# Exponentials per head straight from PSUM, and transpositions that alternate with first-layer products, in a gated cross-attention and feed-forward kernel

## The reference

```python
x = x + tanh(g_xattn[0]) * attention(layernorm(x), ctx)     # 8 heads of 64, 77 keys
x = x + tanh(g_ffn[0]) * ffn(layernorm(x))                  # 256 -> 1024 -> 256, fixed point

attn = softmax(einsum('bhnd,bhmd->bhnm', q, k) * scale)     # over the 77 keys
def quantized_linear(x, w, b):   # x rounded to 1/16, w and b to 1/64, clipped to 8 bits
    return einsum('bsi,oi->bso', xq, wq) + bq
h = relu(fixed_quant(quantized_linear(x, w1, b1)))
out = quantized_linear(h, w2, b2)
```

## Time and profile before

| | us |
|---|---|
| median of 3 runs (lowest, highest) | 119.74 (119.52, 121.28) |
| the profiled execution's own time | 120.01 |
| its span | 118.2 |
| TensorE busy | 111.8 |
| VectorE busy | 97.7 |
| GpSimd busy | 89.1 |
| ScalarE busy | 76.4 |

### The profile page before, as it was taken

How to read it: one execution, slowest core, us unless ns; L and a number is a source line. 1 busy time by engine, 2 the same in 40 slices (tenths; PEclk the granted TensorE clock), 3 DMA queues, 4 the chain that set the end, 5 groups by cost and what they waited for, 6 DMA issues and landing times.

```text
span 118.2 us, 2898 instructions
## 1 busy us (share of the span) xinstructions
PE 111.8 (95%) x1012; PEld 102.1 (86%) x1012; DVE 97.7 (83%) x223; ACT 76.4 (65%) x169; POOL 89.1 (75%) x161
## 2 busy tenths in 40 slices
PE   7979997899999999999999999999999999999990
PEld 2659976899798999988999999999999999897870
DVE  3029798999999999989999999999797979648981
ACT  4137766869688894998667575748483819448420
POOL 4003587698796989898989978996899999988720
PEclk9999999999999999999999999999999999999999
DMA  4989799300000000000010002000200020020204
GB/s 80 315 247 386 280 375 399 152 0 8 0 3 0 6 3 0 0 6 0 0 74 15 6 0 89 0 3 6 89 0 0 3 89 6 0 89 8 88 13 165
DMA packets 5328, 8.87 MB, mean 75 GB/s; under 512 B 1191, under 2 KB 2242, under 8 KB 5186
## 3 DMA queue, kind: packets, MB, share of 16 engines
q1 hardware_dynamic: 5082, 8.34, 20.1%
q10 hardware_dynamic: 232, 0.34, 0.9%
HBM read 6.59 MB, written 2.10 MB: 73 GB/s over the span
## 4 chain that ended last, share of the span: by engine, by line
PE 52%; POOL 21%; DVE 14%; DMA 5%; issue 3%; ACT 1%; SPq 1%; POOLq 0%; DVEq 0%; ACTq 0%
PE sc_ps L841 15%; PE of_ps L878 12%; PE h_ps L910 7%; DMA wq_sb<-in_L_xattn_Wq_dram 5%; POOL hid L362 5%; POOL x_sb L383 4%; PE of_ps L925 4%; POOL probs L300 4%; POOL rstd L310 3%; POOL yq L316 3%; DVE probs L614 3%; PE tr_ps L853 3%; DVE mx L609 3%; DVE den L621 2%; DVE pT L650 1%
## 5 line engine op out<-in xcount | busy, mean ns | idle before, releaser
L841 PE MATMUL sc_ps<-a_sb,xT 128*128 128x308 f32 x192 | 31.1, 311 | 0.7 <-DVE probs L614 0.7
L878 PE MATMUL of_ps<-u_sb,pT 128*128 128x256 f32 x240 | 30.9, 281 | 0.1
L878 PEld LDWEIGHTS of_ps<-u_sb,pT 128*128 128x128 f32 x240 | 29.5, 188 | 0.3 <-issue 0.3
L841 PEld LDWEIGHTS sc_ps<-a_sb,xT 128*128 128x128 f32 x192 | 27.4, 188 | 1.4 <-issue 1.2
L438 ACT ACTIVATE probs<-probs,rstd 128x616 f32<-128x616 f32 x16 | 13.1, 818 | 23.0 <-DVE probs L614 23.0
L481 ACT ACTIVATE hid_q<-h_ps,b1z 128x256 int8<-128x256 f32 x58 | 24.5, 494 | 3.6 <-PE h_ps L910 3.6
L300 POOL TENSOR_TENSOR probs<-probs,rden 128x616 f32<-128x616 f32 x16 | 19.5, 1221 | 1.9 <-DVE rden L624 1.9
L362 POOL CAST hid<-hid_q 128x512 bf16<-128x512 int8 x27 | 15.8, 611 | 2.0 <-ACT hid_q L481 2.0
L910 PE MATMUL h_ps<-x2T,w1T 128*128 128x256 bf16 x128 | 16.7, 274 | 0.0
L609 DVE TENSOR_REDUCE mx<-sc_ps 128x8 f32<-128x616 f32 x16 | 12.6, 787 | 2.8 <-PE sc_ps L841 2.7
L614 DVE TENSOR_TENSOR probs<-sc_ps,mx 128x616 f32<-128x616 f32 x16 | 12.8, 800 | 0.5
(11 more groups left out here) (124 smaller groups left out, 175.8 us busy)
## 6 DMA issues: line engine op xcount, KB each, us to landing
w_sb<-in_L_ffn_w_dram SPq DMA_DIRECT2D x2, 1024.0 KB, 10.9
out_dram<-x_sb SPq DMA_DIRECT2D x7, 256.0 KB, 2.5
x_sb<-in_x_dram SPq DMA_DIRECT2D x4, 256.0 KB, 8.0
x_sb<-in_x_dram SPq DMA_DIRECT2D x1, 1024.0 KB, 9.8
wq_sb<-in_L_xattn_Wq_dram SPq DMA_DIRECT2D x1, 512.0 KB, 5.8
wv_sb<-in_L_xattn_Wv_dram SPq DMA_DIRECT2D x1, 512.0 KB, 7.8
wo_sb<-in_L_xattn_Wo_dram SPq DMA_DIRECT2D x1, 512.0 KB, 8.6
wk_sb<-in_L_xattn_Wk_dram SPq DMA_DIRECT2D x1, 256.0 KB, 3.4
```

What stands on the lines that cost most here:

```text
L841: ins = nc.tensor.matmul(sc_ps[:, a, 0:HALF], xT[:, T % 2, p, c, :], a_sb[:, q, T // TB, c, HALF * a:HALF * a + HALF], start=first, stop=last)
L878: ins = nc.tensor.matmul(attn_ps, pT[:, T % 2, p, P * c:P * c + P], u_sb[:, q, MC * (T // TB) + c, :], start=first, stop=last)
```

## The change

Two things are changed.

First, from slot 4 on, the five transpositions of `probsT(s)` no longer stand ahead of the eight products of `hidden(s-4)`: a transposition and a product take turns, and the last three products follow together.

Second, for tiles 2 to 15 without 5 (`HEAD_EXP`), VectorE no longer subtracts the maximum. It writes minus maximum times `rstd1` (8 columns), and ScalarE takes the exponential of each head's 77 scores from PSUM with this as bias and `rstd1` as scale, eight activations for a tile. `sc_ps` is then free when the exponentials are done, so `scores` of the next tile waits for `exp_done`. In these tiles `center(s+2)` stands ahead of `stats_first(s+5)` on VectorE, no longer behind it.

```diff
+HEAD_EXP = tuple(T for T in range(2, TILES) if T != 5)
...
             def exponentials(T):
                 act.wait_ge(rstd1_ready, T + 1)
-                act.wait_ge(centered, T + 1)
-                nc.scalar.activation(probs_v(T), probs_v(T), ACT.Exp, scale=rstd1[:, T:T + 1]).then_inc(exp_done, 1)
+                if T in HEAD_EXP:
+                    act.wait_ge(minus_max_ready, T + 1 - centered_by(T))
+                    act.wait_ge(pT_psum, T - 1)
+                    for h in range(H):
+                        ins = nc.scalar.activation(probs_v(T)[:, h, :], sc_v[:, h // 4, h % 4, :], ACT.Exp,
+                                                   bias=minus_max[:, T % 2, h:h + 1], scale=rstd1[:, T:T + 1])
+                    ins.then_inc(exp_done, 1)
+                else:
+                    act.wait_ge(centered, centered_by(T))
+                    nc.scalar.activation(probs_v(T), probs_v(T), ACT.Exp, scale=rstd1[:, T:T + 1]).then_inc(exp_done, 1)
...
+                if T in HEAD_EXP:
+                    dve.wait_ge(rstd1_ready, T + 1)
+                    nc.vector.tensor_scalar(minus_max[:, i, :], mx[:, i, :], rstd1[:, T:T + 1], -1.0, ALU.mult,
+                                            ALU.mult).then_inc(minus_max_ready, 1)
+                    return
...
+                if s + 2 in HEAD_EXP:
+                    center(s + 2)
                 if 1 <= s and live(s + 5):
                     stats_first(s + 5, s + 6)
-                if live(s + 2):
+                if live(s + 2) and s + 2 not in HEAD_EXP:
                     center(s + 2)
...
             def scores(T):
                 pe.wait_ge(xT_high, T + 1)
-                if T >= 1:
-                    pe.wait_ge(centered, T)
+                if T - 1 in HEAD_EXP:
+                    pe.wait_ge(exp_done, T)
+                elif T >= 1:
+                    pe.wait_ge(centered, centered_by(T - 1))
...
-            def hidden(k):
+            def hidden(k, probs_of=None):
                 p, half = k // 2, k % 2
+                if probs_of is not None:
+                    probsT_waits(probs_of)
+                    transposed_chunk(probs_of, 0)
...
-                    ins.then_inc(hid_psum, 1)
+                            if (c, d) == (1, DK - 1):
+                                ins.then_inc(hid_psum, 1)
+                            done = 4 * n + 2 * c + d + 1
+                            if probs_of is not None and done < MC:
+                                transposed_chunk(probs_of, done)
...
-                probsT(s)
+                if s >= 4:
+                    hidden(s - 4, probs_of=s)
+                else:
+                    probsT(s)
```

More of the change, by code:

```diff
@@ L123, in flamingo_kernel @@
         mx = sb("mx", [P, 2, H])
+        minus_max = sb("minus_max", [P, 2, H])
         probs_words, probs = words_of("probs", [P, 2, HMP])
@@ L225, in flamingo_kernel @@
         scores_ready, max_ready, centered, exp_done = sem("scores_ready"), sem("max_ready"), sem("centered"), sem("exp_done")
+        minus_max_ready = sem("minus_max_ready")
         den_ready, rden_ready, probs_ready = sem("den_ready"), sem("rden_ready"), sem("probs_ready")
@@ L238, in flamingo_kernel, with centered_by @@
         block = stack.enter_context(nc.Block())
+        def centered_by(T):
+            return len([t for t in range(T + 1) if t not in HEAD_EXP])
         def live(T):
@@ L845, in probsT, with probsT_waits @@
             def probsT(T):
+                probsT_waits(T)
+                for c in range(MC):
+                    transposed_chunk(T, c)
+            def probsT_waits(T):
                 pe.wait_ge(probs_ready, T + 1)
@@ L851, in probsT, with transposed_chunk @@
                 pe.wait_ge(xT_ready, min(T + 3, TILES))
[L852 to L855, removed]
+            def transposed_chunk(T, c):
+                ins = nc.tensor.transpose(pT_ps[:, P * c:P * c + P].bitcast(F32R), probs_words[:, T % 2, P * c:P * c + P],
+                                          ident_r[:, :])
+                if c == MC - 1:
+                    ins.then_inc(pT_psum, 1)
             def attend(T):
@@ L887, in quantisedT @@
                 else:
-                    pe.wait_ge(centered, TILES)
+                    pe.wait_ge(exp_done, TILES)
                     if T - 2 in yT_last:
@@ L1022, in _ @@
                     output_weights(1)
-                if s >= 4:
-                    hidden(s - 4)
                 if s == 5:
```

## The result

The changed kernel takes 131.64 us (median of 4 runs, 130.87 to 134.52) against 119.63 before: 1.099 times the time, 95% interval 1.094 to 1.104. The forecast was slower, 126.3 us, range 122.0 to 129.5. The direction was right, and so was the circle that the prediction describes (maximum, exponentials, denominators, next maximum); the size was not: the loss is 12.0 us, forecast 6.7.

The account below looks back on a forecast made before the run. TensorE bounds the kernel from 36.45 to near 80 us, VectorE before, GpSimd after to 109.0; the change closes a circle. 120.01 + 6.5 (13 steps 6.1, tail 0.4) = 126.5, median 126.3 us, range 122.0 to 129.5.

Parts of the forecast that it names:

- the circle: VectorE and ScalarE, from one tile's maximum through exponentials and denominators to the next maximum: 6.2 us a slot against 5.82.
- The price of the exponentials: ScalarE, one exponential of 77 columns with two per-partition operands: 456 ns, the next following after 0.33 us.
- E: ScalarE's time for the eight exponentials of a tile: 2.7 us against 0.81, 2.3 to 3.0 held likely.
- The early circle: The circle in early slots, with no second-layer result in the slot: 5.83 us against 5.11.
- four of the five shrink: TensorE, alternating slots: four transpositions hide their weight load behind products and shrink to some 55 ns, 0.12 us a slot.
- 0.16 for the new one: VectorE's new 8-column operation, minus maximum times rstd: 0.16 us, bounds nothing and twice that.
- 1.8 us of product: TensorE's score products between exponentials and next maximum: 0.05 + 1.8 us, less than VectorE's 0.09 + 1.95.
- ScalarE's own load does not bind: ScalarE's work of a slot grows from 3.8 to 5.7 us, under the new slot of 6.2 us.
- 13 steps: The steps from the maximum of tile 2 to that of tile 15: 78.1 us against 72.02, +6.1 us.
- The tail behind the last maximum: After tile 15's maximum, exponentials end 1.25 us later, partly under GpSimd's backlog: 0 to 1.25 us more, taken as 0.4.
- cheap: Rival: E near 1.8 us, circle 5.3 us under TensorE's 5.8, about 120 us, no change; chance 0.13.
- dearer: Rival: exponentials overlap by only 0.09 us, E = 3.0 us, 130 us, or 128.3 at half the step; chance 0.22.

Follow-up runs that it names:

- e8: The changed kernel, but tiles 2 to 15 without 5 subtract no maximum and take one exponential of 616 columns per tile; 119.21 us, ratio 0.993.
- e5: As e4, but the exponentials take a constant as scale, leaving one per-partition operand (computes something else, good for time alone); 121.71 us, ratio 1.013.
- e10: As e4, but without the alternation of transpositions and products; 128.12 us, ratio 1.061.
- e6: As e4, but the statistics of a later tile stand ahead of the centring again; 131.71 us, ratio 1.095.
- e7: The changed kernel plus 8 and 6 TensorE products nobody reads, ahead of its waits in slots 1 and 3; 130.79 us, ratio 1.088.
- e4: The changed kernel, but the 8 maxima of a head tile go to spare PSUM columns; 127.0 to 127.8 us in three executions, ratio 1.068.
- e1: The changed kernel measured again without an edit, beside its variants; 133.87 us, ratio 1.122.
- e3: The changed kernel without the alternation, exponentials per head kept; 131.75 us.
- e9: As e4, but tile 7 keeps its old course, centred by VectorE with one exponential; 126.86 us, 125.2 and 125.3 at clock 1.000.
- e2: The kernel before with only the alternation of transpositions and products, all exponentials as before; 119.98 us, ratio 1.002.

## Why the prediction was wrong

**What bounds the kernel** was right: e8 takes 19 us of VectorE's load away, and 0.8 us come back.

**The price of the exponentials.** Forecast 456 ns for one, spacing 0.33, E = 2.7 us; measured 427 ns, 0.305 and 2.56. The error is −0.14 us a tile, 1.8 us in all, and in the kernel's favour. The Trainium skill, page "ScalarE: Activation LUTs", section "What ACT_TABLE_LOAD costs", has 93 ns for an operand, near the 84 measured (e5); one exponential by its figures takes 436 ns, an estimate and near the 427. Its overlap of 93 ns is less than the 122 measured (427 − 305), so E by its figures, 2.84, was too long.

**The circle** was right: 6.13 us where nothing disturbs it (e10), forecast 6.2; it reacts to E (e5) and to work put into it (e6). The early circle, 5.83 by forecast, took 5.78 and 5.83 us at full clock (e7), and there luck helped: from maximum to denominators 3.73 and 3.75 us instead of 3.88, back to the maximum 2.05 and 2.08 instead of 1.95. At full clock and without the wait for GpSimd the kernel takes 127.0 to 127.8 us (e4), where the forecast said 126.3.

**The alternation** was forecast at 0.12 us a slot; it is 0.03. The step "four of the five shrink" failed: transpositions do follow closer, the products behind them later. It cost nothing, as the forecast gave it nothing on the path.

**What failed** are three assumptions of the sum:
- The price "0.16 for the new one", with bounds nothing and twice that. Measured 0.23 undisturbed and up to 1.52, some 3.1 us in all (e7 to e4). I priced it by an operation of one column in the tail of the kernel before, which took 154 ns although GpSimd was adding beside it:

```profile
107.04 0.15 DVE L742 TENSOR_SCALAR ve<-mv 128x1 f32<-128x1 f32 x1
```

```profile
106.83 0.73 POOL L383 TENSOR_TENSOR x_sb<-x_sb,b_gated 128x256 f32<-128x256 f32 x1
```

So the nearest row of before did not show the wait. The Trainium skill has a rule for it, page "SBUF — State Buffer", section "Who interferes with whom": some VectorE instructions and GpSimd's take the same port in turn, and the later one waits for the whole of the other. The rows agree in the main: with the input in PSUM the wait is gone, and all seven durations of 0.40 us and more in e1 end 0.02 to 0.03 us after the end of a GpSimd instruction (65.90 and 65.87). Two things do not fit it. The 1.52 us run past the end of two GpSimd instructions to that of the third. And beside a GpSimd instruction of 2 columns (line 303, 71.35 to 72.07) the operation took 0.23, as if alone. Why is open. The rule would have widened this bound to the length of GpSimd's instructions at least.
- That TensorE runs at full clock, which the prediction takes for granted. The prediction has "1.8 us of product" behind the exponentials, less than VectorE's way; at the lower clock it took 2.60, and then TensorE is the later one. The clock fell after waits of 1.97 and 1.52 us in the early slots, which the change itself made: 3.1 us (e1 to e7), 2.8 by e3's executions, 2.5 in the traces.
- "ScalarE's own load does not bind." True for slots 6 to 12, whose work I had summed. Slot 5 also holds two weight copies of 2.0 us together, and tile 7's exponentials start 1.35 us late (e9).

The sum closes in e7's trace, which is at full clock. Its 13 steps take 81.7 us against 78.1 forecast. Of these 3.6 us the wait for GpSimd has 2.9 and the step from tile 7 to 8 (7.58 in e10 against 6.2, the backlog) 1.4; the other steps lie 0.7 below the forecast, mostly by the shorter E. The tail behind the last maximum takes 23.4 us against 22.3 before, where the forecast added 0.4, so 0.7 more. That makes 126.3 + 3.6 + 0.7 = 130.6, and e7 measured 130.8. The clock's 3 us on top make e1's 133.9. The first measurement, 131.6, lost less to the clock (0.985 to 0.987 against 0.973).

The rival "cheap" did not come true: E was 2.56 with two operands. Nor did "dearer", although the measured time lies above even its 130: E was shorter than forecast, and the loss came from elsewhere.

## What to carry to other kernels

Splitting one instruction into eight pays the fixed part eight times (0.81 to 2.56 us here), and the engine that has idle time for it may still put its length on a circle: follow the consumer's order, not the busy share. A wait is priced by what it does to others: in e1 two waits of TensorE, of 1.5 and 2.0 us, went with another 2.5 to 3.1 us lost to the lower clock. And an operation on 8 columns is as long as what its engine has to wait for. So look at what GpSimd does at that moment, and do not trust a row of another shape for it; here letting the maxima lie in spare PSUM columns took the wait away (e4).

## What the runs showed of the hardware

- A second per-partition operand costs an activation 84 ns (427 against 343 ns, 77 columns from PSUM); back to back, 0.12 to 0.13 us of each is hidden (spacing 0.305 and 0.214).
- An 8-column VectorE operation from SBUF to SBUF took 0.23 to 1.52 us beside GpSimd (e1), from PSUM to SBUF 0.225 to 0.228 us in every tile of e4, e5, e6, e9 and e10.
- A fp32 transposition of 128 columns between bf16 products of 256: 0.19 us a pair (e2), against 0.084 + 0.111 = 0.195 in blocks.
- TensorE's clock fell to its lower level after waits of 1.5 to 2.0 us in the early slots, in some executions of e3 and not in others (granted clock 0.973 and 0.997); filled waits kept it at 1.000 in four of four (e7).
- One execution of e4 had a mean granted clock of 0.666 and took 158.7 us, where its neighbours took 127.0 to 127.8; the cause is open.
